# Projection of a cross-attention block: key weights split early, a short last context chunk, mask tiles looked through in two places, loops written out

## What is computed

```python
q = x @ Wq + bq;  k = ctx @ Wk + bk;  v = ctx @ Wv + bv        # Wq 1024x1024, Wk and Wv 1024x256
scores = einsum('bkgld,bksd->bkgls', q, k) / sqrt(32) + mask   # mask (4, 1, 1024, 1601), here all zero
out = einsum('bkgls,bksd->bkgld', softmax(scores), v) -> (b, l, 1024) @ Wo + bo
x = out + x
return (x - mean(x)) / sqrt(var(x) + 1e-6) * gamma + beta
```

## Time and profile before

| | us |
|---|---|
| median of 3 runs | 3845.93 (3843.28 to 3846.05) |
| the profiled execution, its own time | 3848.16 |
| its span in the profile | 3846.5 |
| projection stage in it | about 0 to 770 |
| attention, then output | about 771 to 3470, then to the end |

### The profile page before, as it was taken

The page is one execution under the profiler, slowest core; times in us unless marked ns, Lnnn a source line. Parts: engine busy times, 40 slices in busy tenths (PEclk is TensorE's granted clock), DMA queues, the critical chain, the costliest instruction groups (busy, mean ns, idle before and its releaser), DMA issues. The chain is left out here.

```text
span 3846.5 us, 54629 instructions
## 1 busy us (share of the span) xinstructions
PE 3776.4 (98%) x20306; PEld 2381.8 (62%) x20306; DVE 2504.1 (65%) x2918; ACT 2034.1 (53%) x3865; POOL 2888.6 (75%) x1104
## 2 busy tenths in 40 slices
PE   8999999999999999999999999999999999999998
PEld 7998877755555555555555555555555555537886
DVE  3334555377777777777777777777777777735765
ACT  2222122136666666666666666666666666661110
POOL 1111111139999999999999999999999999994555
PEclk9999999979999999999999999999999999999999
DMA  5335677437667667767767667767767767667764
GB/s 177 136 139 181 222 264 249 156 65 157 146 143 158 146 144 154 149 143 158 146 144 157 145 144 156 148 143 156 147 143 157 146 145 156 152 163 212 203 190 125
DMA packets 297548, 612.08 MB, mean 159 GB/s; under 512 B 132064, under 2 KB 169056, under 8 KB 264800
## 3 DMA queue, kind: packets, MB, share of 16 engines
q0 software_dynamic: 58080, 337.15, 38.9%
q1 hardware_dynamic: 235968, 265.54, 26.1%
q10 hardware_dynamic: 3264, 6.29, 0.5%
HBM read 244.50 MB, written 96.99 MB: 89 GB/s over the span
## 5 line engine op out<-in xcount | busy, mean ns | idle before, releaser
L1027 DVE TENSOR_REDUCE half_max<-score 128x1 f32<-128x800 f32 (+1 forms) x2048 | 1893.4, 985 | 712.3 <-PE score L882 708.8
L1086 ACT ACTIVATE weights<-logit 128x512 f32<-128x512 f32 (+1 forms) x3328 | 1732.5, 603 | 801.2 <-PE logit L927 772.4
L802 POOL TENSOR_TENSOR sum_pool<-sum_pool,weights 128x2048 f32<-128x2048 f32 x446 | 2124.9, 4764 | 34.0 <-ACT weights L1086 6.4
L882 PE MATMUL score<-qk_store 96*128 96x400 f32 (+1 forms) x4096 | 1208.7, 377 | 14.0 <-issue 9.1
L927 PE MATMUL logit<-qk_store 98*128 98x512 f32 (+1 forms) x3328 | 1201.2, 417 | 7.6 <-ACT weights L1086 5.4
L882 PEld LDWEIGHTS score<-qk_store 96*128 96x128 f32 x4096 | 688.3, 191 | 551.1 <-DVE half_max L1027 424.9
L937 PE MATMUL mixed<-weights,v_sb 128*32 128x512 f32 x6656 | 809.9, 601 | 0.7 <-ACT weights L1086 0.7
L927 PEld LDWEIGHTS logit<-qk_store 98*128 98x128 f32 (+1 forms) x3328 | 607.9, 185 | 271.2 <-ACT weights L1086 135.8
L937 PEld LDWEIGHTS mixed<-weights,v_sb 128*32 128x32 f32 x6656 | 177.4, 109 | 393.7 <-ACT weights L1086 219.7
L802 POOL TENSOR_TENSOR sum_pool<-weights 128x2048 f32<-128x2048 f32 x64 | 313.6, 4900 | 49.4 <-ACT weights L1086 49.4
L514 POOL DMA_DIRECT2D q_parts<-o_hi x64 | 34.5, 539 | 311.5 <-DMA q_parts<-o_lo 214.5
(11 more groups left out here) (84 smaller groups left out, 2695.1 us busy)
## 6 DMA issues: line engine op xcount, KB each, us to landing
weights<-weights POOLq DMA_DIRECT2D x191, 1024.0 KB, 7.2
sum_pool<-weights POOLq DMA_DIRECT2D x63, 1024.0 KB, 7.0
qk_store<-q_parts SPq DMA_DIRECT2D x192, 256.0 KB, 3.9
qk_store<-k_parts SPq DMA_DIRECT2D x192, 200.1 KB, 5.6
rows<-in_ctx SPq DMA_DIRECT2D x26, 1024.0 KB, 5.2
landing<-in_mask_Bx1xSxS_ff SPq DMA_DIRECT2D x32, 800.5 KB, 7.1
rows<-in_x SPq DMA_DIRECT2D x16, 1024.0 KB, 6.3
q_parts<-o_hi POOLq DMA_DIRECT2D x64, 256.0 KB, 2.8
```

The lines of the kernel that those rows point to most:

```text
L802: nc.gpsimd.tensor_tensor(sum_pool[s % 2][0:w], first[0:w], weights[buffer(s, st)][0:w], ALU.add).then_inc(pool_added, 1)
L882: last = nc.tensor.matmul(score[j][:, c, 0:w], q_sb[buf][0:STACK, h, lt * P:(lt + 1) * P], k_sb[buf][0:STACK, start:start + w], start=True ...
L1027: nc.vector.tensor_reduce(half_max[m // NROW % 2][:, k % G, k // G, j:j + 1], score[j][:, :, 0:HALVES[j][2]], mybir.AxisListType.XY, ALU.m ...
L1086: nc.scalar.activation(weights[buffer(s, st)][0:w, h, :], logit[u % BANKS][0:w, :], ACT.Exp).then_inc(exp_done, 1)
```

## The change

In words:

- **Start.** ScalarE and VectorE split Wk after the first four slices of chunk 0, then the other four slices, then Wv. TensorE waits for Wk at the first key sum and for Wv at the first value sum.
- **Last context chunk.** It takes 3 row tiles (384 rows) and computes 260 key columns and three value sums. Turning it takes 3 transposes a slice. The last chunk has five groups.
- **Mask.** Context chunks 1 to 8 look through two tiles each, after their sums 2 and 5; the x chunks take 3, 3, 2, 2, 2, 2, 2, 0. The first three pieces of Wq, which were loaded at the start into the same slots, are loaded at the end of context chunk 9.
- **Loop.** All 13 context chunks are written out on all engines.
- **End.** GpSimd doesn't wait for the last two pairs of query stores; SyncE waits for them in `attend`, behind its first load. `landing`, `full`, `o_hi` and `o_lo` lie in `mask_store`, which is now there in both stages.

```diff
-    BESIDE = {"x": [(t,) for t in range(KT)], "ctx": [(0, 1), (2, 3), (4,), (5,), (6,), (7,)]}
+    BESIDE = {"x": [(t,) for t in range(KT)], "ctx": [(0, 1), (2, 3), (4,), (5,), (6,), (7,)], "last": [(0, 1), (2, 3), (4,), (5,), (6, 7)]}
+    LAST = B * S - (NCC - 1) * XC
+    LT = -(-LAST // P)
+    LG = KG + LT
+    SUMS = (NCC - 1) * CG + LG
     HALF = H // 2
-    MASKS = (5, 5, 5, 5, 4, 4, 4, 0)
-    assert sum(MASKS) == MT and len(MASKS) == NXC
+    MASKS = (0, 2, 2, 2, 2, 2, 2, 2, 2) + (0,) * (NCC - 9) + (3, 3, 2, 2, 2, 2, 2, 0)
+    assert sum(MASKS) == MT and len(MASKS) == NCC + NXC
...
     def mask_turns(c):
-        return [(i + 1) * XG // MASKS[c] - 1 for i in range(MASKS[c])]
+        groups = len(beside(c))
+        return [(i + 1) * groups // MASKS[c] - 1 for i in range(MASKS[c])]
...
+        return BESIDE["last" if u == NCC - 1 else "ctx" if u < NCC else "x"]
+
+    def short(kind, c):
+        return kind == "ctx" and c == NCC - 1
+
+    def row_tiles(u):
+
+        return LT if u == NCC - 1 else XC // P
+
+    def key_cols(c):
+
+        return slice(LT * P - LAST, LT * P) if c == NCC - 1 else slice(0, XC)
...
+        return B * S - LT * P if c == NCC - 1 else c * XC
...
-    def all_chunks(engine, step):
-
-        with engine.Fori(0, NCC // 2 - 1) as i:
-            for par in range(2):
-                step("ctx", i * 2 + par, par)
-        for c in range(NCC - 3, NCC):
+        return kind == "x" and c == NXC - 1
+
+    def all_chunks(step):
+
+        for c in range(NCC):
             step("ctx", c, c % 2)
         for c in range(NXC):
             step("x", c, (c + NCC) % 2)
...
+        full = [mask_store[:, 2 * S + (4 + i) * XC:2 * S + (5 + i) * XC] for i in range(2)]
+        o_hi, o_lo = [[mask_store[:, 2 * S + (2 * n + i) * XC:2 * S + (2 * n + i + 1) * XC].bitcast(F32R) for i in range(2)] for n in range(2)]
         v_out = [v_store[:, i * KV:(i + 1) * KV] for i in range(2)]
 
-        landing = sb("landing", [P, 2 * S])
+        landing = mask_store[:, 0:2 * S]
...
-        W_RUNS = (range(KVW), range(KVW, KVW + 3), range(KVW + 3, KVW + 6), range(KVW + 6, len(w_pieces)))
+        W_RUNS = ((), range(KVW, KVW + 3), range(KVW + 3, KVW + 6), range(KVW + 6, len(w_pieces)))
...
-                sp.dma_start(rows[:, :, cols], src[bass.ds(first, XC), cols].rearrange("(t p) h -> p t h", p=P)).then_inc(rows_in[half], 16)
+                cols, n = slice(half * HALF, (half + 1) * HALF), row_tiles(u)
+                sp.dma_start(rows[:, 0:n, cols], src[bass.ds(first, n * P), cols].rearrange("(t p) h -> p t h", p=P)).then_inc(rows_in[half], 16)
 
             def load_mask(tile):
+                if tile == 0:
+                    sp.wait_ge(w_lo_done, KVW)
+                if tile == sum(MASKS[:NCC]):
+                    sp.wait_ge(w_lo_done, len(w_pieces))
...
+                following = ("x", 0) if short(kind, c) else (kind, c + 1)
                 if kind == "ctx":
                     for half in range(2):
                         load(*following, half)
+                    for tile in mask_tiles(c):
+                        load_mask(tile)
...
-                if turns:
-                    sp.wait_ge(w_lo_done, len(w_pieces))
-
...
-                for a in range(XC // P):
+                for a in range(row_tiles(u)):
...
+                    if u == 0 and g in (0, KG):
+                        pe.wait_ge(w_lo_done, KVW // 2 if g == 0 else KVW)
...
+                        keys = key_cols(u)
+                        three(acc[:, 0:keys.stop - keys.start], [(w[:, t, cols], m[:, t, keys]) for w, m in ((w_hi, hi), (w_hi, lo), (w_lo, hi)) for t in range(KT)])
...
-            pe.wait_ge(w_lo_done, KVW)
-            with pe.Fori(0, NCC // 2 - 1) as i:
-                for par in range(2):
-                    step("ctx", i * 2 + par, par)
-            for c in range(NCC - 3, NCC):
+            for c in range(NCC):
                 step("ctx", c, c % 2)
...
-                    if kind == "ctx" and isinstance(c, int) and g == 2:
+                    if kind == "ctx" and c >= NCC - 3 and g == 2:
                         split_weights_hi(W_RUNS[c - NCC + 4])
...
-                if kind == "ctx" and isinstance(c, int) and c < NCC - 1:
+                if kind == "ctx" and NCC - 4 <= c < NCC - 1:
+                    if c == NCC - 4:
+                        act.wait_ge(mask_sized, 2 + sum(MASKS[:NCC]))
                     load_weights(W_RUNS[c - NCC + 5])
 
-            for t in range(KT):
+            for t in range(KT // 2):
                 split_hi(0, t, 0)
-            split_weights_hi(range(KVW - LAND))
+            split_weights_hi(range(KVW // 2))
+            for t in range(KT // 2, KT):
+                split_hi(0, t, 0)
             load_weights(range(LAND, KVW))
-            split_weights_hi(range(KVW - LAND, KVW))
-            load_weights(W_RUNS[1])
+            split_weights_hi(range(KVW // 2, KVW))
             act.wait_ge(bias_in, 48)
             act.wait_ge(bias_done, 1)
...
-                    if kind == "ctx" and isinstance(c, int) and g == 2:
+                    if kind == "ctx" and c >= NCC - 3 and g == 2:
                         split_weights_lo(W_RUNS[c - NCC + 4])
...
-                    if kind == "x" and g in mask_turns(c):
-                        look_through(mask_tiles(c)[mask_turns(c).index(g)])
-
-            for t in range(KT):
+                    if g in mask_turns(u):
+                        look_through(mask_tiles(u)[mask_turns(u).index(g)])
+
+            for t in range(KT // 2):
                 split_lo(0, t, 0)
-            split_weights_lo(W_RUNS[0])
+            split_weights_lo(range(KVW // 2))
+            for t in range(KT // 2, KT):
+                split_lo(0, t, 0)
+            split_weights_lo(range(KVW // 2, KVW))
...
                 for g in range(XG if kind == "x" else KG):
                     pool.wait_ge(part_lo, p0 + (g + 1))
...
-                            dst = k_dram[n, g * P:(g + 1) * P, bass.ds(start(c), XC)]
-                        pool.dma_start(dst, part[g % 2][:].bitcast(F32)).then_inc(part_stored, 16)
-                    pool.wait_ge(part_stored, p0 * 32 + 32 * (g + 1))
-                    pool.sem_inc(part_free[g % 2], 1)
+                            keys = key_cols(c)
+                            w = keys.stop - keys.start
+                            dst = k_dram[n, g * P:(g + 1) * P, bass.ds(start(c) + keys.start, w)]
+                        pool.dma_start(dst, part[g % 2][:, 0:w].bitcast(F32)).then_inc(part_stored, 16)
+                    if not (final(kind, c) and g >= XG - 2):
+                        pool.wait_ge(part_stored, p0 * 32 + 32 * (g + 1))
+                        pool.sem_inc(part_free[g % 2], 1)
                 if kind == "ctx":
-                    for j in range(XC // P):
+                    for j in range(row_tiles(c)):
...
             load_step(0, 0, 0)
+            sp.wait_ge(part_stored, 32 * (NCC * (KV // P) + NXC * KT))
             load_mask_max(0)
```

More of the change, by code:

```diff
@@ L260, in step @@
             def step(kind, c, par):
-                turns = kind == "ctx" and isinstance(c, int) and c == NCC - 1
-                following = ("x", 0) if turns else (kind, c + 1)
+                following = ("x", 0) if short(kind, c) else (kind, c + 1)
                 if kind == "ctx":
@@ L273, in step @@
                         load_ahead()
-                    tiles, pieces = mask_tiles(c), wo_pieces(c)
+                    tiles, pieces = mask_tiles(NCC + c), wo_pieces(c)
                     for i in range(max(len(tiles), len(pieces), 2)):
@@ L319, in step @@
                 hi, lo = t_hi[par], t_lo[par]
-                for g, beside in enumerate(BESIDE[kind]):
+                for g, turns in enumerate(beside(u)):
                     if not final(kind, c):
-                        for t in beside:
+                        for t in turns:
                             turn(u + 1, t)
+                    if u == 0 and g in (0, KG):
+                        pe.wait_ge(w_lo_done, KVW // 2 if g == 0 else KVW)
                     if g == 0:
@@ L423, in split_lo @@
                 dve.wait_ge(hi_done, u * KT + (t + 1))
[L424 removed]
+                w = row_tiles(u) * P
+                nc.vector.tensor_tensor(t_lo[par][:, t, 0:w], turned[t % 2][:, 0:w], t_hi[par][:, t, 0:w].bitcast(F32), ALU.subtract).then_inc(lo_done, 1)
             def split_weights_lo(pieces):
@@ L463, in step @@
                         nc.vector.tensor_scalar(flag[:], flag_sum[:], 0.0, None, ALU.not_equal).then_inc(flag_done, 1)
-                    acc = summed[bank(kind, par, g)]
+                    acc = summed[bank(kind, c, g)]
+                    w = key_cols(u).stop - key_cols(u).start
                     if kind == "x" or g < KG:
```

70 lines of the change are left out of this document (33 added, 37 removed).

## The result

| | before, us | after, us |
|---|---|---|
| median of 6 runs each | 3845.99 (3843.28 to 3851.36) | 3823.36 (3820.54 to 3827.25) |
| profiled execution, own time | 3848.16 | 3820.54 |
| its span | 3846.5 | 3818.9 |

The ratio is 0.9939, 95% interval 0.9929 to 0.9950: 22.6 us faster by the medians. The forecast was 28.7 and 3817.2; the time lies inside the range of 3811 to 3831 (its ends as added up were 3812.5 and 3832.5), 6.2 us above the point. So two questions stand: which terms carry the 27.6, and why the medians moved by less.

What follows compares the result with a forecast made beforehand. TensorE, busy 98% of the span, bounds the kernel; gains lie where it idles or does removable work. Terms 6.7 + 9.0 + 11.0 + 2.0 = 28.7 us off 3848.2 give 3819.5, less 2.2 a median of 3817.2; range 3811 to 3831.

Steps and rivals of the forecast that it cites:

- Start: First key sum: needing only Wk it begins 7.0 us earlier, 0.3 lost to late Wv; 6.7 us, between 4.5 and 7.5.
- Last context chunk: Last context chunk: shorter key sums, one value sum and 8 transposes fewer save 9.0 us, between 7.5 and 9.3.
- Mask tiles out of the x chunks: X chunks: fewer mask tiles queued ahead of Wo pieces remove TensorE's t_lo waits; 11.0 of 12.9 us, between 6 and 12.9.
- the fifth: X chunks: t_lo wait from the 12 early loads, 2.87 us plus 1.7 slow clock; VectorE on time should carry it.
- Mask tiles in the context chunks: Context chunks: 16 added looks and loads priced at nothing; up to 3 us if the cover fails in part.
- The cover named: Context chunks: VectorE only 51% busy, DMA 201 GB/s, first tile issued 19 us before it is wanted, so looks cost nothing.
- Loop written out: Context chunk loop: writing it out gains or loses nothing on TensorE, as the row at a loop turn shows no stall.
- End: Between the stages: GpSimd not waiting for its last stores gains 2.0 us, only 0.2 if the barrier still drains them.
- The x waits stay: X chunks: a Wo piece's own store and reload plus the early loads cause the waits; gain 19.7, 3826 us; chance 0.16.
- The clock doesn't fall: Between the stages: TensorE stays at 2.4 GHz across a gap of about 7 us; 3811 us; chance 0.05.
- The looks hold TensorE: Context chunks 1 to 8, sums 2 and 5: unlanded tiles stall TensorE; at 3 us a look, 3865 us; chance 0.04.
- Part is given back: Context chunks: a pinch of 1 us a chunk, and one at the short last chunk; 3829 us; chance 0.08.

Runs made afterwards that it cites:

- wv_slot: Changed kernel with Wv's second piece given its own landing place and loaded at the start, not after the eight slices; 3824.37 us, ratio 0.9941.
- start_undone: Changed kernel with the old start order: Wk and Wv split after all eight slices, TensorE waiting for all four pieces; 3824.71 us, ratio 0.9944.
- long_last: Changed kernel with the last context chunk back at 512 rows and six sums; 3830.57 us, ratio 0.9958.
- masks_back_2: Second profile of the changed kernel with all 32 mask tiles put back in the x chunks; 3834.57 us, one run.
- before_again: The kernel before, unchanged, run once more for a second profile; 3843.26 us, one run.
- the kernel called both: Changed kernel with Wv's second piece in its own landing place and the last two query store pairs issued by SyncE; 3817.06 us, ratio 0.9921.

## Why the prediction was right, and where not

**Start: mis-sized.** Forecast 6.7, measured 5.4. The first sum was right to 0.2 us and the next late thing was named. The step that failed is "its second piece is loaded at the same time as before ... is cast at about 24 to 24.5". It was issued at 18.89, 0.01 us after 1 MB of rows, and needed 6.7 us, so it was cast at 25.66. Before it was issued at 19.99, 2.7 us behind those rows, and needed 4.0. I took before's landing time for a transfer that met the rows at another moment: both are released by the split, and the split had moved. wv_slot, without that wait, gets the loss back. At the key sum of chunk 1, where the 5.4 was read, the order by itself is worth 4.7 (start_undone). The other 0.7 lies between start_undone and before, which have the same order at the start, and was not separated; two more profiles of the old start have 61.11 and 61.32 there, where before has 61.43.

**Last context chunk: right.** Forecast 9.0, measured 9.3 with 0.3 of closer spacing, and 9.0 in long_last. The sum at 260 columns, scaled to 2.97, takes 24 x (337.97 - 335.94) / 16 = 3.05 us by the timeline of masks_back_2:

```profile
335.94 1.22 PE L331 MATMUL summed<-t_hi,qk_store 128*128 128x260 f32 x8
336.99 1.14 PE L331 MATMUL summed<-t_lo,qk_store 128*128 128x260 f32 x8
337.97 1.14 PE L331 MATMUL summed<-t_hi,qk_store 128*128 128x260 f32 x8
```

That is 127 ns a matmul, where the scaled row gave 124; by the rows the two key sums saved 5.3, not 5.4. The scaled row was the better price than the 111 ns that the prediction took from the Trainium skill ("TensorE: Matmul & The Clock Gate", Back-to-back issue gap). That page gives the formula for a matmul by itself and says that in a stream with weight loads it under-counts at small widths and over-counts at large ones, so it wasn't the price of such a stream, as the prediction took it to be.

**Mask tiles out of the x chunks: right in sign, wrong in size and in part of the mechanism.** Forecast 11.0. All waits went, the fifth too; the forecast left 1.9 of the 12.9 standing. Against the profile of before that gave 12.5. Against the mean of five profiles it gives 9.8. The step that failed is the first: 12.9 us of excess were read off one execution and taken for the kernel's. The 2.2 us by which that execution lay above the median were then taken off the starting time, but not off the term. But before and before_again differ by 4.9 in their spans and by 4.1 of that in the x stage, so the excess that lifts an execution above the median is for the most part the one that the term already takes away: it was counted twice. Right was that VectorE isn't full and that ScalarE's 79 us for Wo come from what stands around the pieces. Half right was the part played by the order: a piece issued ahead of the tile does land sooner (4.5 against 7.0 us), but then the tile is late, so the tile *ahead of* the piece is not the whole cause. With all the tiles in these chunks one of the two is late.

**Mask tiles in the context chunks: next to nothing, as forecast, but not in every execution.** The cover named was for the looks, and they hold TensorE in no profile. The hole is elsewhere: a value store that goes out just behind rows and a tile, which cost 5.2 us around one chunk of long_last, more than the 3 us that the forecast allowed. In the other profiles with tiles there, 0.1 to 0.5 us are lost around one chunk, and nothing in start_undone. Since masks_back_2 shows such a loss without tiles in the context chunks, the tiles aren't its only cause. That it makes after's runs spread by 7 us is possible, and was not shown. A third value buffer was not tried.

**Loop written out: nothing, right.**

**End: mis-sized.** Forecast 2.0, measured 0.95. The text named both cases, 2.0 and 0.2 "if the barrier itself still drains the stores", and took the wrong one: the barrier drains them, only from an earlier start, which is why more than 0.2 is left.

**The rivals.** The x waits stay: no, 377.28 in seven profiles. The clock doesn't fall: it did, in a gap of 8.13 and even in one of 5.06 (granted clock 0.50, the 1.2 GHz level, at 745 to 750 in after and in the kernel called both). The looks hold TensorE: no. Part is given back: not by the looks; the 0.6 us of attention and output are within what profiles differ by.

**The sum.** Profile against profile, 27.6 came of 28.7: start -1.3, last chunk +0.3, x chunks +1.5, end -1.05, attention -0.6. That these nearly cancel is luck: the x chunks gave more than forecast only because they were measured against an execution with much to lose. The medians moved by 22.6, or 26.3 beside each other on a second chip, since before's profile was high for its kernel, above all in its x chunks, and after's was low. The 6.2 us by which the forecast median was missed are, to 0.1, 1.1 from the terms, the 2.2 that were taken off on top of them, and 2.8 by which after's profile lies below the median of its runs. Where a slower run of after loses these 2.8, no profile on record shows.

## To carry to other kernels

Waits that depend on which transfers meet differ from one execution to the next: read a second profile before you size a term on their sum, and don't take an execution's excess over the median off once more when it is already in a term. Where two transfers are both late, changing their order moves the wait; taking traffic out of the stage removes it (here 377.28 us against 385 to 390). A wait taken out before a barrier is only worth what the barrier doesn't wait for by itself; move the store to an engine whose end is not drained for it.

## What the hardware showed

- GpSimd's drain at the end of a block took 1.29 us when its own stores had landed and 3.2 when they had not; the gap between the stages is 9.04, 8.13 and, with the stores on SyncE's queue, 5.06 us. SyncE's drain took 0.12 us right behind the issue of such stores.
- A store of 128 KB landed in 2.4 us (median in after), but the six looked at (in six kernels) that were issued within 3 us behind 1 MB of rows and 0.8 to 1 MB more took 5.4 to 8.0.
- TensorE's clock fell to its lower level in a gap of 5.06 us too, and stayed there for some 58 us (738.0 to 796.0 in the kernel called both), as in the kernel before (768.1 to 826.2). Behind the wait of 2.65 us in masks_back_2 it was at 0.50 from 343 to 345 us and back at 1.00 by 347.
